# First layer of groups two to four: the first two output tiles computed whole, behind all mixing steps, instead of in token halves

## The reference, cut to what matters

```python
W = weights[condition]                                   # one 64x64 matrix per batch
mixed = einsum('bct,bcd->bdt', x, W)                     # mixes the 64 tokens of a batch
x = x + (mixed @ W_base.T + b_base + adapter(mixed))     # first layer
h = silu(lora(x, gate)) * lora(x, up)                    # second layer, 2752 wide
down = lora(h, down)
x = x + (down @ sign(weight).T + bias)
```

## Time and profile before

| what | value |
|---|---|
| time, three runs | 1940.18, 1940.35, 1941.18 us; median 1940.35 |
| time of the profiled execution | 1939.93 us |
| its span, first to last instruction | 1938.2 us, so 1.73 us lie around it |
| busy PE / DVE / ACT / POOL | 99% / 77% / 39% / 28% of the span |
| mean granted TensorE clock | 0.998 of 2.4 GHz |

### The profile page before, as it was taken

How to read it: one execution, slowest core, us unless ns; L and a number is a source line. 1 busy time by engine, 2 the same in 40 slices (tenths; PEclk the granted TensorE clock), 3 DMA queues, 4 the chain that set the end, 5 groups by cost and what they waited for, 6 DMA issues and landing times.

```text
span 1938.2 us, 31467 instructions
## 1 busy us (share of the span) xinstructions
PE 1912.8 (99%) x9088; PEld 1605.7 (83%) x9088; DVE 1493.0 (77%) x2484; ACT 763.3 (39%) x1450; POOL 543.9 (28%) x935
## 2 busy tenths in 40 slices
PE   6999999999999999999999999999999999999998
PEld 5888888888988888888898888888889888888887
DVE  6977777778778777777777877777877787777786
ACT  3453333334344343333344434333335443334331
POOL 6442222213415212211523322212071322222100
PEclk9999999999999999999999999999999999999999
DMA  9675445543476554444447655454334655555411
GB/s 245 152 147 108 103 98 116 121 94 82 126 149 127 106 115 100 101 99 88 119 116 143 124 113 110 106 116 99 70 102 131 139 121 110 121 110 113 99 44 44
DMA packets 320629, 219.43 MB, mean 113 GB/s; under 512 B 177192, under 2 KB 311208, under 8 KB 320544
## 3 DMA queue, kind: packets, MB, share of 16 engines
q1 hardware_dynamic: 281952, 189.47, 43.5%
q0 software_dynamic: 36352, 24.19, 7.0%
q10 hardware_dynamic: 2240, 4.72, 0.7%
HBM read 205.40 MB, written 12.58 MB: 112 GB/s over the span
## 4 chain that ended last, share of the span: by engine, by line
PE 92%; DVE 4%; issue 2%; ACT 2%; DMA 0%; POOLq 0%; DVEq 0%; ACTq 0%; POOL 0%
PE ps L1404 26%; PE ps L1406 26%; PE ps L1405 26%; PE ps L1611 6%; PE ps L1538 2%; PE ps L1458 2%; PE ps L1459 2%; DVE ps L876 2%; PE ps L1430 1%; PE ps L1477 1%; PE ps L1428 1%; DVE split L862 1%; ACT split L608 0%; ACT hidden L608 0%; PE ps L1648 0%
## 5 line engine op out<-in xcount | busy, mean ns | idle before, releaser
L1404 PE MATMUL ps<-x,split 128*128 128x512 f32 x1376 | 537.7, 391 | 1.3 <-DVE split L862 1.3
L1406 PE MATMUL ps<-x,split 128*128 128x512 f32 x1376 | 536.3, 390 | 0.0
L1405 PE MATMUL ps<-x,split 128*128 128x512 f32 x1376 | 535.4, 389 | 0.0
L608 ACT ACTIVATE split<-ps 128x512 fp32r<-128x512 f32 x344 | 203.0, 599 | 450.8 <-DVE ps L876 438.8
L505 POOL DMA_DIRECT2D nat_ad<-L_cond_A_down x224 | 137.3, 620 | 733.4 <-DVE ps L876 724.3
L1406 PEld LDWEIGHTS ps<-x,split 128*128 128x128 f32 x1376 | 258.3, 188 | 55.8
L1405 PEld LDWEIGHTS ps<-x,split 128*128 128x128 f32 x1376 | 258.4, 188 | 54.8
L1404 PEld LDWEIGHTS ps<-x,split 128*128 128x128 f32 x1376 | 259.0, 188 | 50.0 <-DVE split L862 2.5
L1404 PE MATMUL ps<-hidden 128*128 128x512 f32 x672 | 261.5, 389 | 0.0
L1405 PE MATMUL ps<-hidden 128*128 128x512 f32 x672 | 261.5, 389 | 0.0
L1406 PE MATMUL ps<-hidden 128*128 128x512 f32 x672 | 261.4, 389 | 0.0
(11 more groups left out here) (137 smaller groups left out, 2830.5 us busy)
## 6 DMA issues: line engine op xcount, KB each, us to landing
nat<-L_cond_W_gate SPq DMA_DIRECT2D x336, 128.0 KB
nat<-L_cond_W_up SPq DMA_DIRECT2D x336, 128.0 KB
nat_down<-L_cond_W_down SPq DMA_DIRECT2D x112, 384.0 KB, 6.4
nat_a<-L_ffn_weight SPq DMA_DIRECT2D x128, 128.0 KB, 2.8
nat<-effective_weight SPq DMA_DIRECT2D x24, 512.0 KB
nat<-x SPq DMA_DIRECT2D x16, 512.0 KB
nat_b<-L_cond_B_gate POOLq DMA_DIRECT2D x224, 24.0 KB, 2.2
nat_b<-L_cond_B_up POOLq DMA_DIRECT2D x224, 24.0 KB, 2.1
```

The source lines that it names most:

```text
L608: act.activation(dst, src, func).then_inc(piece_hi, 1)
L1404: pe.matmul(dst, a[0], b[0], start=first, stop=False)
L1405: pe.matmul(dst, a[0], b[1], start=False, stop=False)
L1406: return pe.matmul(dst, a[1], b[0], start=False, stop=last)
```

## The change

In groups two to four tiles 0 and 1 are no longer done in halves. The two calls inside and behind the mixing steps are gone; the tiles are now done whole, by `first_layer(g, 0)` and `first_layer(g, 1)`, when all eight steps have been issued. Tile 0 takes over the waits that the second half had: step 6's rest ahead of chunk 0 and step 7's rest ahead of chunk 4. The first group (g = 0, `making`) keeps its halves.

```diff
@@ first_layer @@
                 for k in range(KC):
-                    if half == 1 and k % 4 == 0:
+                    if (half == 1 or (half is None and u == 0)) and k % 4 == 0:
                         pe.wait_ge(mixed_lo, 8 * g + 7 + k // 4)
                         pe.wait_ge(xt_copied, 8 * g + 7 + k // 4)
@@ mixing_all @@
                     mixing(g, e, before)
-                    if e == 6 and before is not None:
-                        first_layer(g, 0, 0)
-                if before is not None:
-                    first_layer(g, 1, 0)
@@ first_layer_all @@
                 if making:
                     first_layer(g, 0, 0)
-                first_layer(g, 0, 1)
+                    first_layer(g, 0, 1)
+                else:
+                    first_layer(g, 0)
@@
                     if u == 1:
                         if making:
                             first_layer(g, 1, 0)
-                        first_layer(g, 1, 1)
+                            first_layer(g, 1, 1)
+                        else:
+                            first_layer(g, 1)
```

## The result

| | before | changed |
|---|---|---|
| time, median of ten runs | 1940.2 us (1939.25 to 1941.32) | 1944.83 us (1943.21 to 1946.39) |
| profiled execution | 1939.93 us, span 1938.2 | 1944.69 us, span 1943.0 |

The ratio is 1.0022, with a 95% interval of 1.0015 to 1.003: the change makes the kernel slower, by an amount at the edge of what a measurement of it can tell. The prediction was 1943.9 us, in a range of 1942.2 to 1945.7, with most of its chance on "no difference", close to the edge; the result came out just beyond that edge.

A forecast was written before the change was run, and what follows sets the result against it. PE's queue of matmuls plus its standstills was taken to bound the kernel. Losses of 1.20 + 1.16 + 1.19 = 3.55 us on the profiled 1939.93 gave 1943.5, plus 0.42 for the median: 1943.9 us, range 1942.2 to 1945.7.

The forecast's parts named there:

- no difference: The whole kernel's time differing from before by no more than about 0.2%, here 3.9 us; chance 0.69.
- The gain: Tiles 0 and 1, groups two to four: 48 pairs merged, 12.5 ns saved each, 0.60 us a group.
- The standstill: Group two: PE idle 0.20 us before step 7 and 1.40 us before tile 0, plus 0.10 each restart.
- The row for L1428: A new PE wait before step 7, three times, about 0.05 us to 0.2 us, expected in the profile after.
- The sum: Losses of groups two to four, 1.20 + 1.16 + 1.19 = 3.55 us; bounds 2.2 and 4.2 us.
- No absorption: PE's later 0.33 us wait at 611.25 stays, so nothing is given back; other bound 1.0 us back.
- a rival on the pace: Whole tiles behind mixing run at the pace of two halves: 1.80 us lost a group, 1945.7 us; chance 0.02.
- the clock: Clock halves for about 6.9 us at each new standstill: up to 3.4 us more a group, 1954.2 us; chance 0.06.
- slower by over 0.2%: Whole kernel slower by more than 3.9 us; chance 0.30, of which 0.20 from the prediction's own case.

The follow-up runs named there:

- the filled one: The changed kernel with filler matmuls in PE's two gaps of group one: median 1943.23 us, 4.40 more than the kernel before with the same fillers.
- the two filled comparisons: Fillers in group one in both kernels: changed 1943.23 against before 1938.83 us; and, with the changed kernel's standstills also filled, 1941.99 against 1938.33 us.

## Why the prediction was right, and what it missed

- *The gain.* 0.60 us a group from the wide matmuls was right: tile 1 alone, whole against halves, made 55.90 into 55.59, 12.9 ns for each of its 24 pairs. Of the two prices for a pair, 12.5 ns from the earlier trace rows and 2.5 ns as an estimate from the Trainium skill's page "TensorE: Matmul & The Clock Gate", section "Back-to-back issue gap", the trace's holds. That section gives the formula for a matmul by itself and says that a stream of weight loads and matmuls, as this one, follows other figures (131 ns at 512 columns, where this trace has 226.9). So the prediction should not have taken the formula as a price for this stream; none of these figures of the page agrees with it.
- *The standstill.* Step 6's rest was to stay where it was, and did, to 0.02 us. Tile 2 was to begin 533.47 - 509.35 = 24.12 us behind the first mixing matmul; it began 534.75 - 510.63 = 24.12 behind. Inside this sum three terms were a little off and cancel: the rest came 0.02 us earlier, PE started 0.10 us behind it instead of 0.06, and the next matmul came after 0.31 instead of 0.33. That the sum agrees to 0.01 us is luck; that it agrees to 0.1 is not. The row for L1428 that I named did not appear in PE's waits; the 0.2 us show only in the 0.34 us between the starts of 520.50 and 520.84.
- *What sets it.* That most of it is the weight unit ahead of step 6's copies was shown by moving it (0.99 of 1.17 us), and the cover that the first halves gave by putting them back, in part or whole.
- *The sum.* 3.55 us was forecast, 3.50 was found in the stages. No absorption was right as well. But the medians differ by 4.63 us, more than the 4.2 that the sum allowed at most: the measured time lies inside the stated range because that range also took in the spread of the runs and a rival on the pace, not because a term for the clock was in it.
- *The term that was mis-sized* is the clock. The prediction put it as all or nothing, 0.06 for 3.4 us in every group. In fact it falls at some of the standstills: in none of three in the profile of the changed kernel, in one of three in the filled one, and costs 1.6 us each time, since the stretch at half clock was 3.4 us long, not 6.9. With one of six, an estimate from few cases, that is 3 x 1.6 / 6 = 0.8 us on the mean, and the two filled comparisons, each with its own base on its own chip, differ by 4.40 - 3.66 = 0.74. This brings 3.5 to about 4.3 and moves the ratio from 1.0018 to the measured 1.0022. By this estimate the chance for "slower by over 0.2%" should have been nearer to a half than 0.30.
- *What stays open.* In the unfilled kernels the medians differ by 4.63 us, and the rest of 1.1 is not divided. The record says that it goes with the clock: of the ten runs of the changed kernel the three at a mean clock of 0.998 took 1943.21 to 1943.98 us, the five at 0.997 took 1944.58 to 1945.41, and the two at 0.996 took 1946.04 and 1946.39; none of the 60 runs of the kernel before beside the filled kernels is under 0.997. It does not say where in a run the clock was low. Falls at standstills and a longer half-clock stretch in group one can both be in it, and only one execution of each kernel has a profile. Nor does any run show why the clock falls at one standstill of 1.28 us and not at the next.

## What to carry to other kernels

Small matmuls at a boundary can be cover and not waste: before they are merged, write down when the data of the next consumer is ready and what PE will do until then; here 0.6 us of efficiency was paid for with 1.8 us of standstill and restart. Cover just enough: five of eight chunks in halves keep two thirds of the gain and leave no wait. And a standstill of PE in a dense stream can have a price beyond its length, so it deserves a chance of its own for each place, not one for all.

## What the runs showed of the hardware

The granted clock fell to 0.50 behind a standstill in which PE was idle for 1.28 us in one stage out of six, and behind 2.1 us in three out of three; PE had been nearly dense before and was dense after. It did not fall behind 0.54 to 0.56 us (three stages) or 0.48 us (three stages), nor when the 1.3 us were filled with matmuls. Each time it stayed at 1.2 GHz for 3.4 us, with 512-column matmuls 0.43 us apart instead of 0.23, and cost 1.6 us.

In group one, where PE runs the same instructions in all eight unfilled kernels, the stretch at half clock was 6.8 us long in four profiles (the kernel before is one) and 10.2 in the other four (the changed kernel is one). From the group's own first mixing matmul to its end it took 78.2 to 78.3 us in the first four and 79.6 to 79.8 in the others. Filled with 34 small matmuls, whose work nobody needs, it took 76.8 to 77.1 in six profiles, and the whole kernel before became 2.6 to 2.8 us faster.
